# Four graph-network layers on one core: row maxima stored in four masked blocks, subtracted by 512-column matmuls

## The reference

```
layer 0: q,k,v = x@Wq.T+bq, ...          8 heads of 32
         logits = q.k/sqrt(32) + log(clip(adj,1e-8));  attn = softmax(logits)
         x = layer_norm(x + (attn@v)@Wo.T+bo)*gamma+beta
layer 1: fp = x@fc_w.T+fc_b;  logits = q_i + k_j, masked by adj, leaky slope 0.01
         x = softmax(logits)@fp + x
layer 2: as layer 0 with a term a_i + c_j and log(adj+1e-9), no output projection
         x = softmax(scores)@v + x
layer 3: as layer 1
```

## Time and profile before

| | before |
|---|---|
| median of 3 runs | 1814.74 us (1814.38 to 1816.23) |
| profiled execution: time, span | 1811.3 us, 1809.5 us |
| PE, PEld busy | 1750.8 us (97%), 1642.0 us |
| DVE, ACT, POOL busy | 1474.9, 1371.8, 731.3 us |
| granted TensorE clock, mean | 0.987 of 2.4 GHz |

### The profile page before, as it was taken

How to read it: one execution, slowest core, us unless ns; L and a number is a source line. 1 busy time by engine, 2 the same in 40 slices (tenths; PEclk the granted TensorE clock), 3 DMA queues, 4 the chain that set the end, 5 groups by cost and what they waited for, 6 DMA issues and landing times.

```text
span 1809.5 us, 68658 instructions
## 1 busy us (share of the span) xinstructions
PE 1750.8 (97%) x28065; PEld 1642.0 (91%) x28065; DVE 1474.9 (82%) x3361; ACT 1371.8 (76%) x3792; POOL 731.3 (40%) x797
## 2 busy tenths in 40 slices
PE   6899999999999999999999999999999999999985
PEld 6799999999999999999999999999999999999974
DVE  4678888888888888888888888888888888888873
ACT  3577787787787787787877778778778777778773
POOL 3344443443444344344344344444444344344321
PEclk8999999999999999999999999999999999999997
DMA  3011111011011011011011011111111101101100
GB/s 108 28 37 37 37 49 48 26 49 49 26 49 49 26 49 48 26 49 49 27 47 49 30 44 49 38 37 49 34 40 49 49 26 49 47 28 49 35 13 18
DMA packets 48260, 74.55 MB, mean 41 GB/s; under 512 B 5456, under 2 KB 21968, under 8 KB 47952
## 3 DMA queue, kind: packets, MB, share of 16 engines
q1 hardware_dynamic: 47376, 69.49, 12.0%
q10 hardware_dynamic: 576, 0.68, 0.2%
HBM read 53.37 MB, written 16.78 MB: 39 GB/s over the span
## 4 chain that ended last, share of the span: by engine, by line
PE 88%; ACT 3%; DMA 2%; DVE 2%; issue 2%; POOL 2%; SPq 0%; POOLq 0%; DVEq 0%; ACTq 0%
PE banks L911 16%; PE banks L976 14%; PE banks L913 14%; PE banks L912 14%; PE banks L1125 7%; PE banks L1020 6%; PE banks L1011 6%; PE banks L999 3%; DMA x_t<-x_t_dram 2%; PE banks L1025 2%; PE banks L1085 2%; PE banks L1119 2%; PE banks L1113 2%; POOL weights_B L486 1%; PE banks L985 1%
## 5 line engine op out<-in xcount | busy, mean ns | idle before, releaser
L486 POOL TENSOR_TENSOR weights_B<-weights_B,adj 128x512 f32<-128x512 f32 x64 | 115.2, 1801 | 297.4 <-ACT weights_B L567 297.4
L492 POOL TENSOR_TENSOR inv_parts_A<-inv_both_A,own 128x512 fp32r<-128x512 f32 x64 | 66.6, 1041 | 305.0 <-DVE inv_both_A L835 305.0
L800 DVE TENSOR_REDUCE least_cols_A<-banks 128x4 f32<-128x512 f32 x256 | 159.0, 684 | 32.4 <-PE banks L976 32.3
L800 DVE TENSOR_REDUCE least_B<-banks 128x4 f32<-128x512 f32 x256 | 173.2, 681 | 13.6 <-PE banks L985 13.6
L911 PE MATMUL banks<-w_hi_v,xt_hi 128*128 128x258 f32 (+1 forms) x512 | 157.4, 308 | 13.2 <-DVE w_lo_v L677 11.5
L911 PE MATMUL banks<-w_hi_f,xt_hi 128*128 128x258 f32 x512 | 163.5, 319 | 3.0 <-DVE xt_lo L677 1.5
L641 ACT ACTIVATE fp<-banks 128x258 f32<-128x258 f32 x256 | 92.1, 390 | 93.8 <-PE banks L913 93.8
L567 ACT ACTIVATE banks<-banks,v_B 128x256 f32<-128x256 f32 x384 | 153.7, 475 | 0.0
L911 PE MATMUL banks<-xt_hi,w_hi_k 128*128 128x256 f32 x512 | 151.7, 296 | 0.0
L913 PE MATMUL banks<-w_lo_f,xt_hi 128*128 128x258 f32 x512 | 146.3, 286 | 0.0
L1125 PE MATMUL banks<-fpt,fp 128*128 128x128 f32 x1024 | 143.5, 283 | 2.8 <-ACT fpt L662 2.7
(11 more groups left out here) (192 smaller groups left out, 6210.4 us busy)
## 6 DMA issues: line engine op xcount, KB each, us to landing
x_t<-x_t_dram SPq DMA_DIRECT2D x64, 256.0 KB, 3.6
x_in<-x_dram SPq DMA_DIRECT2D x64, 256.0 KB, 3.6
out_dram<-x_out SPq DMA_DIRECT2D x64, 256.0 KB, 2.4
adj_t<-adj_t_dram SPq DMA_DIRECT2D x64, 128.0 KB, 3.4
adj<-adj_dram SPq DMA_DIRECT2D x64, 128.0 KB, 2.0
scratch<-weights_dram SPq DMA_DIRECT2D x9, 256.0 KB, 6.9
scratch<-weights_dram ACTq DMA_DIRECT2D x2, 256.0 KB, 4.6
out_bias<-L_gnn_bo_dram ACTq DMA_DIRECT2D x1, 128.0 KB, 6.9
```

Of the source, the lines that this page charges most:

```text
L486: pool.tensor_tensor(units, units, weight_of[where][:, G.four, :, :].unsqueeze(2).broadcast_to([P, GROUP, 2, P]), ALU.mult).then_inc(first ...
L800: dve.tensor_reduce(to, bank[SCORE_BANKS[n]].rearrange("p (u m) -> p u m", u=UNITS), axis=AX.X, op=ALU.min).then_inc(maxed[where], 1)
```

## The change

`turn_max`'s copy on ScalarE becomes four copies. Copy u multiplies by column u of `pick` ([128 x 4], 1 on partitions 32r+u, else 0), so `least_rows` is now [128, 4, 128] with the maxima of unit u alone in block u. `shift` then is one matmul for each head r: all 32 rows of the row group, a stationary matrix of -1 (`minus`), 512 moving columns; 4 instead of 16. The number of columns that are streamed is the same. The table `ORDER` is laid out anew: the turn begins at another place of the cycle (`den` of A instead of `k` of layer 0), which changes all lags and the assignment of banks, and within the cycle some steps change places.

```
-    act.activation(least_rows[where][:, :], bank[b][:, 0:P], ACT.Copy)
+    for u in range(UNITS):
+        last = act.activation(least_rows[where][:, u, :], bank[b][:, 0:P], ACT.Copy,
+                              scale=pick[:, u:u + 1])
...
-    for u in range(UNITS):
-        for r in range(HALF):
-            part = row_group(r, UNITS)
-            last = pe.matmul(bank[SCORE_BANKS[r]][:, cols(u)], minus_pick[part, u, :],
-                             least_rows[s][part, :], start=False, stop=True, ...)
+    for r in range(HALF):
+        part = row_group(r)
+        last = pe.matmul(bank[SCORE_BANKS[r]], minus[part, :],
+                         least_rows[s][part, :, :].rearrange("p u n -> p (u n)"),
+                         start=False, stop=True, ...)
...
 "gpsimd":
-    (1, "weigh", "A", 0), (1, "den", "A", 0), (3, "weigh", "B", 0), (1, "penalty", "", 0), (1, "rstd", "", 0), ...
+    (1, "den", "A", 0), (3, "weigh", "B", 0), (0, "bias", "0", 0), (0, "penalty", "", 0), (1, "rstd", "", 0), ...
```

More of the change, by code:

```diff
@@ L27 @@
     "tensor": [
[7 rows of a table removed]
-    "vector": [
[6 rows of a table removed]
-        (0, "out_proj", "0", 0), (2, "weigh", "B", 2), (2, "weigh", "B", 3), (-1, "adj_t", "", 0),
-        (0, "out_proj", "0", 1), (3, "inv", "3", 0), (0, "norm", "", 0), (-1, "max", "A", 0), (-1, "max", "A", 1)],
-    "scalar": [
[8 rows of a table removed]
[8 rows of a table added]
+    "vector": [
+        (1, "split", "A", 0), (-1, "adj_t", "", 0), (3, "weigh", "B", 1), (3, "weigh", "B", 2),
+        (1, "out_proj", "0", 0), (3, "weigh", "B", 3), (1, "out_proj", "0", 1), (4, "inv", "3", 0),
+        (0, "max", "A", 0), (1, "norm", "", 0), (0, "max", "A", 1), (0, "max", "A", 2), (0, "max", "A", 3),
[5 rows of a table added]
+    "scalar": [
[9 rows of a table added]
     "gpsimd": [
-        (0, "turn_x", "0", 0), (0, "bias", "0", 0), (4, "den", "B", 0), (4, "bias", "3", 0), (1, "weigh", "A", 0),
-        (1, "den", "A", 0), (3, "weigh", "B", 0), (1, "penalty", "", 0), (1, "rstd", "", 0), (-1, "adj_t", "", 0)],
+        (0, "adj_t", "", 0), (1, "den", "A", 0), (3, "weigh", "B", 0), (0, "bias", "0", 0), (0, "penalty", "", 0),
+        (1, "rstd", "", 0), (-1, "turn_x", "0", 0), (3, "den", "B", 0), (3, "bias", "3", 0), (0, "weigh", "A", 0)],
     "sync": [
@@ L170, in build_kernel @@
         least_cols = {s: sb(f"least_cols_{s}", [P, HALF, HEAD_DIM]) for s in "AB"}
-        least_rows = {s: sb(f"least_rows_{s}", [P, P], F32R) for s in "AB"}
+        least_rows = {s: sb(f"least_rows_{s}", [P, UNITS, P], F32R) for s in "AB"}
         heads = {s: sb(f"heads_{s}", [P, GROUP, DIM]) for s in "AB"}
@@ L576, in turn @@
                         act.wait_ge(filled[b], turn.after(G, *key))
-                        act.activation(least_rows[where][:, :], bank[b][:, 0:P], ACT.Copy).then_inc(rows_ready[where], 1)
+                        for u in range(UNITS):
+                            last = act.activation(least_rows[where][:, u, :], bank[b][:, 0:P], ACT.Copy,
+                                                  scale=pick[:, u:u + 1])
+                        last.then_inc(rows_ready[where], 1)
                     elif name == "use":
@@ L995, in shift @@
                 pe.wait_ge(rows_ready[s], G.no + 1)
-                for u in range(UNITS):
-                    for r in range(HALF):
-                        part = row_group(r, UNITS)
-                        last = pe.matmul(bank[SCORE_BANKS[r]][:, cols(u)], minus_pick[part, u, :],
-                                         least_rows[s][part, :], start=False, stop=True, skip_group_check=True)
+                for r in range(HALF):
+                    part = row_group(r)
+                    last = pe.matmul(bank[SCORE_BANKS[r]], minus[part, :],
+                                     least_rows[s][part, :, :].rearrange("p u n -> p (u n)"),
+                                     start=False, stop=True, skip_group_check=True)
                 last.then_inc(filled[SCORE_BANKS[0]], 1)
```

## The result

| | before | changed |
|---|---|---|
| median | 1814.56 us (1808.79 to 1816.23, 4 runs) | 1852.91 us (1848.47 to 1854.51, 4 runs) |
| profiled execution: time, span | 1811.3, 1809.5 us | 1848.47, 1846.7 us |
| typical turn (median of the turns from 100 to 1700 us) | 26.80 us | 27.45 us |

The changed kernel is slower, ratio 1.0212 (95% interval 1.0193 to 1.0231). Forecast were 1782 us, and 1765 to 1805 as the range.

A forecast was written before the change was run, and what follows sets the result against it. TensorE was taken as the bound, a turn being the sum of its steps. Terms summed to -0.45 us a turn, -28 us over 63 turns; with -7 and +2, 1778 profiled, median 1782 us, range 1765 to 1805.

The forecast's parts named there:

- (a), the mask: At mask of layer 1, TensorE waits for VectorE's addition to the projections: 0 to 0.18 us a turn, taken as +0.08.
- The shift's size: Four 512-column matmuls take 0.30 us to the next step, saving 0.29 per shift, plus 0.09 of A's wait.
- upper bound: Longest time given for the new shift: 0.245 + 384 columns at 2.4 GHz (0.16) = 0.41 us.
- Ahead of B's shift: On TensorE, wide leads into the scores and not into mix, saving one start of a step: -0.05 us (0 to -0.1).
- The order on TensorE: v between A's scores and use of B adds one change of array shape: +0.19 us a turn (0.1 to 0.25).
- The copies: ScalarE's four copies end 1.14 us after the first starts (0.75 to 1.33), just fitting before both shifts.
- A's fit: At A's shift, the copies are done at 6.17 us, 0.1 before TensorE comes at 6.27.
- The late input: Transfer of x_t is issued earlier, with some 9 us of margin, ending the waits: -7 us in all (0 to -8).
- Filling and emptying: At the pipeline's ends, longer copies on an uncovered chain and shorter shifts: +2 us (-4 to +6).
- rival 4: Little or no gain because the new order stalls elsewhere by 0.5 us a turn: about 1814 us; 4% chance.
- The rival for slower: Four ScalarE copies take longer, so TensorE waits at both shifts every turn: 1835 us, or near 1820; 4% chance.
- The signs of being wrong: In the changed kernel's timeline: a shift of 0.6 us or more, copies over 1.4, or a turn over 26.6.

The follow-up runs named there:

- e4: Changed kernel with GpSimd's bias of layer 3 moved behind weigh of B and adj_t ahead of weigh of A: 1823.04 us, ratio 1.0053.
- e7: Changed kernel, orders kept, with VectorE's addition to layer 1's projections reading them from PSUM instead of SBUF: 1826.23 us, ratio 1.0083.
- e6: Changed kernel with each shift as 8 matmuls of 256 columns instead of 4 of 512: 1854.81 us in one run.
- e1: Changed kernel's new ORDER with the old single copy and the old 16 matmuls of the shift: 1868.45 us, ratio 1.0309.

## Why the prediction was wrong

- **What bounds the kernel** was right: a turn is the sum of TensorE's steps, and its waits are the rest.
- **The step that failed is (a), the mask.** It was named as a narrow place and given +0.08 (0 to 0.18) by working out when the addition could start; its duration, 0.15 in the earlier trace rows, was carried over as a constant. The addition, with two inputs from SBUF, stands still while GpSimd reads there (0.62 us instead of 0.15), and the new order brings `bias` of layer 3 beside it. e4 and e7 take that away in two different ways and win 30 and 27 us. Of the +0.74, 0.46 are this (0.82 in the changed kernel, 0.36 in e4). The other 0.26 are the queue, which I had bounded at 0.18: the addition stands behind a `weigh` and starts at the moment at which TensorE is there (745.43, with `turn_rows` at 745.38).
- **The shift's size was wrong too:** 0.43 us against the 0.30 taken and the 0.41 of the upper bound. That the row groups overlap was right, but not how far. The 0.30 leaned on `wide` in the earlier trace rows, 0.23 us, which uses the whole array and is followed by its like; the end of four row tiles of 512 columns is 0.41. The upper bound came within 0.02, by a rule that does not hold in between: for the last four of 256 columns it gives 0.245 + 0.053 = 0.30, and e6 shows 0.22. A row at hand told more: `column_terms` in the earlier trace rows, 0.42 for two fours of 256 columns, is 0.21 for each against 0.115 at 128 columns, so the time of a four grows with its columns. The saving is 0.25 and 0.16 instead of 0.38 and 0.29. The figure in the Trainium skill ("TensorE: Matmul & The Clock Gate", "Measured speedup vs the span model") also gave 0.30, an estimate for the four tiles alone; the 0.43 measured here contains the way into the next step, and no run shows the four without it.
- **Ahead of B's shift** I forecast -0.05 and it was +0.11: `wide` now leads from 512 columns into row tiles at 0.41 us instead of 0.23 into its like, a price that I had not charged.
- **The order on TensorE** was right: +0.19 for one more change of shape, measured +0.18. The rule of "TensorEngine Tiling (Array Packing)" in the Trainium skill, section "Key Properties", that a change of mode drains TensorE, fits what is seen here: from the last matmul to the next step 0.20 us behind `den`, where the shape changes, and 0.09 behind `use`, where it does not (128 columns); 0.41 and 0.23 behind `wide` (512).
- **The copies** were right in size (1.14 us), and e1 shows that they don't slow anything at the mask. A's fit missed by 0.05. B's held: the shift came 1.58 us behind `turn_max` (756.58 - 755.00), not 1.50.
- **The late input** was right: no wait for `x_t`, and mean and median of the turns, 26.93 and 26.80 before, are 27.46 and 27.45 after, which is the 7 us. That it was `penalty`'s place that did it was not tested by itself. **Filling and emptying:** 1811.3 + 63 x 0.65 - 7 = 1845.3, and the profiled execution took 1848.5: +3 where +2 was said.
- **The rivals:** the loss is nearest to rival 4, an order that stalls elsewhere by 0.5 us a turn, at 0.66 in place of 0.5. It had 4% and the time it gives, about 1814, was level, since it stood beside a shift that was counted too cheap by 0.26 a turn. The rival for slower was built on the copies and did not happen. The real one, VectorE and GpSimd in each other's way, was missing, though the lists of steps of both engines in the new order were at hand, the two instructions are 0.01 us apart in the kernel before, and one row of its trace has the addition at 0.93 us.
- **The signs of being wrong:** of the three that were named, only the turn came (27.45, over 26.6). The shift at 0.43 lay between its forecast and its sign.
- **Two sums of the prediction** are off and decide nothing: 4 x 0.39 is 1.56, not 1.58, and a shift that saves 0.18 instead of 0.29 costs 14 us more, not 18 (the 1795 beside it is right).

Open: how the 0.41 us behind 512 columns divides between columns that still stream and a change of the array's shape. The runs show the sum alone.

## What to carry to other kernels

When instructions change places, lay VectorE's instructions with two SBUF inputs, and its tensor_scalars from SBUF to SBUF, beside GpSimd's in the new order, and charge each pair that meets with the whole rest of the earlier one; a duration from the old trace holds only for its old neighbours. Look at the longest instance of a row too, not only at its median. Price a matmul by what follows it: the same whole-array matmul of 512 columns costs 0.23 us ahead of a like shape and 0.41 ahead of row tiles. And where a change needs a new order to be covered at all, run the order alone: here it cost 54 us, and the shift brought back 16.
